# The maximum over all partitions taken from GpSimd to TensorE and VectorE, and ScalarE's tables loaded ahead of use, in a fused attention and feed-forward kernel

## What is computed

```python
x = x + conv_ref(_ln_c(x), ...)            # sim = sigmoid(beta + alpha*cos); keep the argmax center
t = _to_tokens(x)
t = t + ffn_ref(_ln_t(t), W1, b1, W2, b2)
# ffn_ref:
def _quantize_activations_groupwise(x):     # called on h and again on the output
    for g in range(NUM_GROUPS):
        ag = x[g*gs:(g+1)*gs]
        gamma = jnp.max(jnp.abs(ag))
        xq = xq.at[g*gs:(g+1)*gs].set(jnp.clip(ag*QB/(gamma+EPS), -QB+EPS, QB-EPS))
h   = quantize(x @ Wb1.T + b1);  h = gelu(h)
out = quantize(h @ Wb2.T + b2)
```

## Time and profile before

| | us |
|---|---|
| median of 3 runs | 3264.39 (3263.29 to 3267.81) |
| span of the profiled execution | 3259.8 |

### The profile page before, as it was taken

The page is one execution under the profiler, slowest core; times in us unless marked ns, Lnnn a source line. Parts: engine busy times, 40 slices in busy tenths (PEclk is TensorE's granted clock), DMA queues, the critical chain, the costliest instruction groups (busy, mean ns, idle before and its releaser), DMA issues.

```text
span 3259.8 us, 72165 instructions
## 1 busy us (share of the span) xinstructions
PE 2986.8 (92%) x20760; PEld 2046.0 (63%) x20760; DVE 2731.3 (84%) x5896; ACT 2271.4 (70%) x4628; POOL 2034.3 (62%) x4668
## 2 busy tenths in 40 slices
PE   3999999989999988999998989999988999998985
PEld 2677776666666655666665566666655666665553
DVE  3788887989988987998887978888887889897966
ACT  1677676967776787777676967767686767677943
POOL 1676675256766755777675757766655777675743
PEclk9999998999999989999998989999988999998977
DMA  1011111012222200222221012222200222120024
GB/s 47 16 31 39 38 33 31 0 45 61 61 65 57 60 16 16 61 61 68 58 64 38 0 47 68 64 58 67 60 2 16 68 68 71 52 68 23 15 72 122
DMA packets 31010, 155.43 MB, mean 48 GB/s; under 512 B 6483, under 2 KB 6676, under 8 KB 30612
## 3 DMA queue, kind: packets, MB, share of 16 engines
q1 hardware_dynamic: 30612, 150.74, 16.7%
HBM read 76.06 MB, written 74.66 MB: 46 GB/s over the span
## 4 chain that ended last, share of the span: by engine, by line
POOL 40%; PE 24%; issue 22%; ACT 7%; DVE 6%; POOLq 1%; ACTq 0%; DVEq 0%; SPq 0%
PE ps L958 5%; POOL eq L452 5%; POOL mo_x L397 4%; PE ps L1033 4%; POOL mo_t L397 4%; ACT turns L588 3%; PE ps L1071 3%; POOL nxy L428 3%; POOL ninv L434 3%; POOL ny L426 3%; POOL mo_x L390 2%; POOL nxy L431 2%; POOL turns L468 2%; PE ps L922 2%; PE ps L966 2%
## 5 line engine op out<-in xcount | busy, mean ns | idle before, releaser
L958 PE MATMUL ps<-wfT,xn 97*112 97x384 f32 x1792 | 734.8, 521 | 39.5 <-issue 21.5
L1033 PE MATMUL ps<-tok,w1T 98*128 (+1 forms) x2880 | 615.1, 338 | 31.8 <-ACT turns L591 29.2
L532 ACT ACTIVATE sq<-ps 112x384 f32<-112x384 f32 x896 | 432.5, 490 | 212.6 <-PE ps L958 208.4
L784 DVE TENSOR_REDUCE hmax<-ps 128x392 f32 (+1 forms) x720 | 394.7, 561 | 72.3 <-PE ps L1033 63.1
L468 POOL CAST turns<-turns 128x392 f16<-128x392 f32 x240 | 319.6, 1348 | 209.2 <-ACT turns L588 200.2
L1033 PEld LDWEIGHTS ps<-tok,w1T 98*128 98x128 f16 x2880 | 282.9, 100 | 236.7 <-issue 54.8
L958 PEld LDWEIGHTS ps<-wfT,xn 97*112 97x112 f32 x1792 | 268.1, 181 | 250.0 <-ACT sq L532 82.0
L704 DVE TENSOR_REDUCE n<-sq 112x32 f32<-112x1536 f32 (+1 forms) x256 | 394.0, 1539 | 13.6 <-issue 8.5
L493 ACT ACTIVATE xnT<-ps,mo_x 112x96 f32<-112x96 f32 x896 | 305.2, 456 | 66.5 <-POOL mo_x L399 66.5
L855 DVE SCALAR_TENSOR_TENSOR turns<-turns 128x1176 f16<-128x1176 f32 x240 | 333.9, 1391 | 0.0
L538 ACT ACTIVATE sig<-cosb,betac 112x896 f32<-112x896 f32 x128 | 133.6, 1044 | 280.1 <-DVE cosb L714 280.0
(11 more groups left out here) (130 smaller groups left out, 6369.3 us busy)
## 6 DMA issues: line engine op xcount, KB each, us to landing
xbuf<-in_x SPq DMA_DIRECT2D x64, 588.0 KB, 4.7
out<-xbuf SPq DMA_DIRECT2D x64, 588.0 KB, 3.7
turns<-out SPq DMA_DIRECT2D x60, 588.0 KB, 6.2
out<-turns SPq DMA_DIRECT2D x60, 588.0 KB, 3.7
cst<-in_constants SPq DMA_DIRECT2D x1, 644.0 KB
tok<-in_L_ffn_W SPq DMA_DIRECT2D x2, 142.5 KB
wf<-in_L_conv_Wf SPq DMA_DIRECT2D x1, 144.0 KB
tok<-in_L_conv_Wv SPq DMA_DIRECT2D x1, 144.0 KB
```

What stands on the lines that cost most here:

```text
L532: nc.scalar.activation(sq[:, t, :], bank(2 + t % 2, TN, D), ACT.Square).then_inc(f_sq, 1)
L784: v.tensor_reduce(o, bank(6 + u % 2, 128, HT), AX.X, ALU.max, apply_absolute_value=True)\
L958: mm(bank(2 + t % 2, TN, D), xn[:, k % 2, t * TN:(t + 1) * TN], wfT[:, :], start=True, stop=True)\
L1033: ins = mm(dst, w1T[:, c * 128:(c + 1) * 128], tok[:, bass.ds(place, 1), part, s * HT:(s + 1) * HT].rearrange("p a n -> p (a n)"), start=p ...
```

## The change

The all-reduce of GpSimd goes, with its two calls per group. In its place TensorE transposes the column `gam[:, i, 0]` into a row in PSUM bank 7 (`column_to_row`), VectorE takes the maximum of that row (`largest_of_row`), and TensorE multiplies a row of ones by this one number, so that every partition gets it (`row_to_column`); `group_scale` reads it from PSUM. Before the second pass the product with ones stands behind the first tile's six products in `up`. Behind the second pass both stand behind the wait for the last `y`, and the second `group_scale` moves from the first `scaled` step of the next pipeline to the end of the group; the first `t` tokens of a group wait for `g_eps`, as bank 7 is theirs too. ScalarE gets two activations of one column into a scratch tile `ahead`: a Gelu before the wait for `g_scale`, and a Sigmoid before the third `y_out` from the end.

```diff
-            def over_partitions(n, i):
-                pool.wait_ge(g_max, n)
-                met()
-                nc.gpsimd.partition_all_reduce(gam[:, i, 1:2], gam[:, i, 0:1], 128, MAX).then_inc(g_all, 1)
...
                 pipeline(pool, g, part, attention)
-                over_partitions(2 * g + 1, 0)
...
                 second_pass(pool, g, [(0, middle_chunk)])
-                over_partitions(2 * g + 2, 1)
...
                 def y_out(k, i, place):
+
+                    if isinstance(place, int) and place == GQ - 2 and k % 2 == 1:
+                        nc.scalar.activation(ahead[:, :], ones[:, 0:1], ACT.Sigmoid)
...
+                nc.scalar.activation(ahead[:, :], ones[:, 0:1], ACT.Gelu)
                 act.wait_ge(g_scale, 2 * g + 1)
                 second_pass(act, g, [(0, gelu), (3, y_out)])
...
+            def largest_of_row(n, i):
+
+                dve.wait_ge(g_T, n)
+                v.tensor_reduce(gam[0:1, i, 1:2], bank(7, 1, 128), AX.X, ALU.max).then_inc(g_row, 1)
+
             def group_scale(n, i):
 
                 dve.wait_ge(g_all, n)
-                v.tensor_scalar(den[:, i, 0:1], gam[:, i, 1:2], EPS_Q, None, ALU.add).then_inc(g_eps, 1)
+                v.tensor_scalar(den[:, i, 0:1], bank(7, 128, 1, 128), EPS_Q, None, ALU.add).then_inc(g_eps, 1)
...
                     if isinstance(place, int) and place == 0:
-                        group_scale(2 * g, 1)
                         dve.wait_ge(g_scale, 2 * g)
...
                 largest(hmax[:, :], 0, 128)
+                largest_of_row(2 * g + 1, 0)
                 group_scale(2 * g + 1, 0)
...
                 largest(ymax[:, :], 1, C)
+                largest_of_row(2 * g + 2, 1)
+                group_scale(2 * g + 2, 1)
                 dve.sem_inc(waited, 1)
...
                         pe.wait_ge(h_max, q * (2 * FC) + START)
+                        if isinstance(place, int) and place == 0 and not (isinstance(g, int) and g == 0):
+                            pe.wait_ge(g_eps, 2 * g)
...
+            def column_to_row(n, i):
+
+                pe.wait_ge(g_max, n)
+                tr(bank(7, 1, 128), gam[:, i, 0:1], ident).then_inc(g_T, 1)
+
+            def row_to_column(n, i):
+                pe.wait_ge(g_row, n)
+                mm(bank(7, 128, 1, 128), ones[0:1, 0:128], gam[0:1, i, 1:2], start=True, stop=True).then_inc(g_all, 1)
...
                     ins.then_inc(bh_ps, 1)
+                    if isinstance(place, int) and place == 0 and k == 0:
+                        row_to_column(2 * g + 1, 0)
...
                 pe.wait_ge(h_max, g * (GQ * 2 * FC) + (START + GQ * 2 * FC))
+                column_to_row(2 * g + 1, 0)
                 second_pass(pe, g, [(0, up), (3, down)])
                 pe.wait_ge(b_y, g * (2 * GQ) + (START + 2 * GQ))
+                column_to_row(2 * g + 2, 1)
+                row_to_column(2 * g + 2, 1)
```

More of the change, by code:

```diff
@@ L73, in build @@
     ALU, ACT, AX = mybir.AluOpType, mybir.ActivationFunctionType, mybir.AxisListType
-    MAX = bass.bass_isa.ReduceOp.max
     ctx = ExitStack()
@@ L122, in build @@
         gam = sb("gam", [128, 2, 2])
+        ahead = sb("ahead", [128, 1])
         den = sb("den", [128, 2, 2])
@@ L195, in build @@
         f_out = [sem(f"f_out{i}") for i in range(2)]
-        g_max, g_all, g_eps, g_rec, g_scale = (sem(n) for n in ("g_max", "g_all", "g_eps", "g_rec", "g_scale"))
+        g_max, g_T, g_row, g_all, g_eps, g_rec, g_scale = (sem(n) for n in ("g_max", "g_T", "g_row", "g_all", "g_eps", "g_rec", "g_scale"))
         w_loaded, pe_set, dve_set, pool_set = sem("w_loaded"), sem("pe_set"), sem("dve_set"), sem("pool_set")
@@ L898, in tile_bank, with to_tokens @@
                 return bank(b0, rows, n, t * n) if t < TA else bank(b0 + 1, rows, n, (t - TA) * n)
-            def to_tokens(s, b0):
+            def to_tokens(s, b0, g=0):
                 def step(k, q, place, use):
@@ L1046, in hidden_tiles, with attention @@
                 return step
-            def attention():
+            def attention(g):
                 return [(M, 1, scores), (A, 1, sim_back(0)), (R, 1, t_back(0), FFN), (A, 1, sim_back(1)),
@@ L1053, in attention @@
                         (X, 1, centers), (A, 1, spread(1)), (M, 0, features(0, 1)), (X, 1, center_products),
-                        (M, 0, features(1, 2)), (R, 0, to_tokens("t", 6), FFN), (M, 0, features(2, 4)),
+                        (M, 0, features(1, 2)), (R, 0, to_tokens("t", 6, g), FFN), (M, 0, features(2, 4)),
                         (X, 1, q_back), (M, 0, features(4, 6)), (A, 0, marks_back), (X, 0, to_tokens("x", 0)),
                         (M, 0, features(6, 7)), (A, 0, find_first)]
+            def column_to_row(n, i):
[4 more added lines that the diff above has]
+                mm(bank(7, 128, 1, 128), ones[0:1, 0:128], gam[0:1, i, 1:2], start=True, stop=True).then_inc(g_all, 1)
             def group(g, part):
-                pipeline(pe, g, part, attention())
+                pipeline(pe, g, part, attention(g))
                 def up(k, i, place):
@@ L1085, in _ @@
                 group(g, "middle")
-            pipeline(pe, GROUPS, "last", attention())
+            pipeline(pe, GROUPS, "last", attention(GROUPS))
 INPUTS = ["x"] + ["L0_conv_" + n for n in ("Wf", "bf", "Wv", "bv", "Wp", "bp", "sim_alpha", "sim_beta")] \
```

## The result

| | before | after |
|---|---|---|
| median, us | 3266.03 (4 runs) | 3211.1 (3207.12 to 3211.35, 4 runs) |
| span of the profiled execution, us | 3259.8 | 3208.8 |
| busy us: TensorE / VectorE / ScalarE / GpSimd | 2986.8 / 2731.3 / 2271.4 / 2034.3 | 2974.6 / 2713.2 / 2257.8 / 1859.6 |

The ratio is 0.9831, 95% interval 0.9818 to 0.9845: 1.7% faster. The forecast was 3217.5 us, the range 3204 to 3238 us. The profiled execution became 51.0 us shorter, the sum had 46.9. The 51.0 us are not made up as the sum said, and the agreement is in large part luck: 20.6 us come from the second passes, where the sum had 6.5 us for the clock, and all the rest gives 30.4 us.

A forecast was written before the change was run, and what follows sets the result against it. Stages were taken as nearly full, with stalls at the seams between pipeline and second pass around GpSimd's all-reduce. Gains 22.8 + 6.5 + 13.1 + 4.5 = 46.9 us off the 3264.39 us median gave 3217.5 us, range 3204 to 3238.

The forecast's parts named there:

- Seam A, term by term: Step from pipeline to second pass: maximum to first Gelu falls to 3.85 us; gain 22.8 us over five groups.
- Seam A, the clock: From pipeline to second pass: TensorE's clock rises earlier after the first Gelu; 1.3 us per group, 6.5 us in all.
- removed at no price: GpSimd's other work goes without gain; L446's 0.37 us and its waits lie on the path already counted.
- Rival (a): The clock gives nothing back: gain only 35.9 us, 3228.5 us; chance 0.2.
- Seam B, groups 0 and 4: Second pass back to pipeline, first and last group: `eq` wait goes, 5.2 and 3.4 us; clock 1.5 us each.
- Seam B, the three groups between: Second pass back to pipeline, at the group loop's jump: 1.5 us each, 4.5 us; clock 0.5 us each.
- the lower branch: At the group loop's jump: TensorE's stop has a fixed length, so it restarts 1.8 us later and 0.6 us remain.
- jumps that grow, since every engine's code is moved: Named among what would make the prediction wrong: loop jumps lengthen because code moves; no size given.
- (b): Clock gives back its upper bounds and middle groups' jumps end with the loads: 57.1 us, 3207.3 us; chance 0.1.
- (c): Stalls come from GpSimd's change between pipeline instructions and the cast, not from the all-reduce; some 3272 us; chance 0.05.
- (d): Table loads stay behind the wait before Gelu, being misplaced: 4 x 1.45 us less gain, 3223.3 us; chance 0.05.
- The signs stated: No GpSimd reconfigurations, maximum to Gelu 3.9 us, `eq` within 0.1 us of `top`, clock rising within 3 us of Gelu.

The follow-up runs named there:

- run 1: Kernel before with only ScalarE's two table loads put ahead of use, maxima still through GpSimd's all-reduce: 3257.97 us, ratio 0.9974.
- run 7: Kernel before, all-reduces kept, with 118 instructions without effect at the start of GpSimd's code: 3236.87 us, ratio 0.9938.
- run 12: Kernel after with 13 unread products filling TensorE's gaps at each pipeline's end, plus 205 instructions without effect at its code's start: 3233.25 us, ratio 0.9907.
- run 9: Kernel after with SyncE's two 588 KB loads of looped groups issued only behind the group loop's jump: 3202.6 us, ratio 0.9816.
- run 8: Kernel after with 16 instructions without effect at the start of TensorE's code: 3197.87 us, ratio 0.9795.
- run 2: Kernel after with GpSimd's all-reduce back behind the second pass, the TensorE path kept only before it: 3238.82 us, ratio 0.9924.
- run 3: Kernel after with the ten all-reduces back on GpSimd at their old places, into a tile nobody reads: 3246.25 us, ratio 0.9947.
- run 6: Kernel after with 10 instructions without effect at the start of GpSimd's code: 3216.19 us, ratio 0.9853.
- run 10: Kernel after with 16 instructions without effect ahead of TensorE's code and SyncE's two 588 KB loads only behind the group loop's jump: 3179.9 us, ratio 0.9762.

## Why the prediction was right, point by point

**In short.** The time was met because an effect that the sum did not hold, 20.6 us, made up for the 16 us by which its terms were too large. Seam A's own terms were right, the 6.5 us of the clock did not come, and from seam B on there were 8.8 us where the sum had 17.6.

**Seam A, term by term: right.** 22.4 us for 22.8, 3.97 us per group for 3.85. In group 1 the product with ones took 0.58 us for 0.35, the six products 2.17 for 2.05; the transpose took 0.37 for 0.53. The hidden row maximum and the table load are as predicted, and run 1 gives 5.4 us for the four loads where the working had 4 x 1.45 = 5.8.

**Seam A, the clock: wrong.** Taken were 1.3 us per group. The step that failed is "so the rise should come earlier as seen from that Gelu", within 3 us of it. The rise came 5.2 to 5.4 us behind the first Gelu in groups 0, 2 and 3, and 8.3 and 7.5 us in groups 1 and 4; before it was 7.0 to 8.4 us. The first four Gelu intervals give back 3.3 us in all five groups (44.6 to 41.3 us). But in just the three groups with the earlier rise the clock fell once more, for 3.4 us, at the end of the pass. Windows of after, group 2, TensorE busy, clock, DMA share, GB/s:

```profile
1744.00:1749.00 5.00, 4.52 (x15) 0.50 0.00 0
1750.00:1752.00 2.00, 2.00 (x14) 1.00 0.00 0
1845.00:1849.00 4.00, 3.68 (x12) 0.57 0.02 4
```

From the fifth interval on these three passes take 98.0 us, the other two 97.1. So the second passes of the kernel after take together 529.6 us from the first Gelu, those of run 7, with all stalls of the all-reduce but no long casts, 528.9: in sum the clock gave back nothing. I took the stall of 6.10 us for what the clock was low for; but it falls ahead of it, in the thin end of the pipeline (1.19 of 4 us busy), which the change leaves as it is. Run 12 shows that this is the place.

**The second pass: not foreseen.** The 20.6 us of that stretch are the long casts. Where the text said that GpSimd is nowhere the busiest and its work is removed at no price, it looked at shares; the row that would have told was the listing of the cast, 1348 ns in the mean for an instruction that takes 0.6 us in group 0. Taken out by run 7, the change is worth 0.9831 / 0.9938 = 0.989 (0.987 to 0.991), some 35 us in the measured times, 26.5 us between the two profiled spans (of different chips), and 30.4 us by the table's other stretches. Rival (a), the clock gives nothing, had 35.9 us. So the forecast of 46.9 us was met by luck: its terms were too large by some 16 us, 6.5 of the clock at seam A and 8.8 from seam B on, and an outside event of 20 us, which the range did not hold by any of its reasons, filled the gap.

**Seam B, groups 0 and 4: the mechanism right, the sizes too large.** From the maximum to TensorE's first use of `eq` it was 11.90 and 10.19 us and is 7.72 and 8.36 us: 4.2 and 1.8 us; to the start of GpSimd's second `eq`, with the clock, 5.9 and 3.4 us. Predicted were 5.2 and 3.4 without the clock, 6.7 and 4.9 with it. In group 0 the clock still falls once: it is 0.50 in the window 668 to 670 and 1.00 from 672 on, where before it was low to 687.

**Seam B, the three groups between: the mechanism right, the choice between the two wrong.** The product with ones ends, and TensorE starts again 6.59, 6.76 and 6.16 us later; before it was 6.72, 6.58 and 6.34 us from the last `y`. The stop has a fixed length and begins 1.9 us later than before. This is the lower branch, 0.6 us per group, and I took 1.5. That the loads lengthen the stop was right as well (run 9), though not as I put it: in group 1 of after the second load landed at 1259.79 and TensorE restarted 2.2 us later, before it landed at 1277.73 and TensorE had restarted 0.8 us earlier. So the restart doesn't follow the end of the loads; why a jump that meets 1.9 us less of them stops as long is not shown. Up to TensorE's first use of `eq` these groups won 1.0, 1.2 and 1.3 us, and up to GpSimd's second `eq` 1.8, 2.1 and 2.5.

**What was lost again: "jumps that grow, since every engine's code is moved".** I named it as what would make the prediction wrong, and left it out of the sum. From GpSimd's `eq` ahead of the inner jump to the one behind it, groups 1 to 4 took 27.82, 26.99, 27.62 and 27.39 us and take 28.34, 29.05, 29.50 and 27.72: 4.8 us lost, over half of the difference between the 15.7 us won near seam B and the 8.8 us of the whole stretch. The rest lies spread over the pipelines; group 0's first stretch alone differs by 7 us between these kernels (554.18 us in run 1, 561.27 in run 8), and I have not found why.

**The rivals.** (b) is out by the clock. (c) is out by runs 2 and 3. (d) is out by the table loads' rows. The signs stated all held for GpSimd, seam A and the jump; the ones for the clock did not.

**Open.** Which instruction of GpSimd comes late, why one late cast is enough in one pass and not in another, and what part the all-reduces have in that (run 3 against run 6), is not shown. That the long casts come of a port shared by GpSimd and VectorE is argued from the rows, and was not tried alone, as by another place for one of L855's inputs.

## What to carry to other kernels

An all-reduce of 0.37 us can stand for 12 to 15 us of program changes around it, and where they are paid depends on which instructions run under either program; look for what waits for the first instruction behind it. An added or removed instruction moves all code behind it: price a loop's jump with the border behind its target, keep big loads out of its way, and if a change gives more than its terms, shift the code of the kernel before by the same amount ahead of believing it. A clock that is low at a stall need not be low because of it: look at the microseconds ahead.

## What the runs showed of the hardware beyond that

- An inner jump costs TensorE 3.1 to 4.1 us. If a code border lies just behind the target, a second stop follows: 1.2 to 2.3 us with eleven products between (before, groups 1 to 4), 1.8 to 3.2 with eight (run 2), 1.8 to 4.1 with four (after, run 9), none with the border ahead of the target (run 8).
- The group loop's jump costs TensorE 6.2 to 6.8 us beside two loads of 588 KB (after), without them 3.3 to 3.9 us (run 9).
- GpSimd starts its all-reduce 5.8 to 6.7 us behind the maximum where a reconfiguration stands ahead of it (before, runs 1, 3 and 7; 7.3 to 8.3 us in run 2), and 0.2 us behind it where none does. The first `eq` afterwards starts 5.6 to 8.0 us behind `top`. A cast needs neither change.
- Instructions without effect take TensorE 0.14 to 0.15 us each where nothing hides them (run 12).
- A second pass can be 4 to 5 us longer by GpSimd's casts alone, once they meet VectorE's two-input instruction, also where GpSimd's code is the same (run 10, group 4 against the others).
